# Second mixture of a two-layer transformer on one core: expert passes with the hidden units on partitions, bias and rectifier in one instruction, second bias by TensorE, expert words kept in registers, deviation per block, 39 blocks

## The reference, cut to what matters

```python
h = relu(einsum('bld,edh->eblh', x, W1) + b1)        # x is the layer-normed input
y = einsum('eblh,ehd->ebld', h, W2) + b2
gate = softmax(x @ gate_W + gate_b);  vals, idx = top_k(gate, 2)
out0 = y of expert idx[0] for x;  out1 = y of expert idx[1] for x + 0.5 * out0
result = layer_norm(x + vals[0] * out0 + vals[1] * out1, gamma, beta, eps=1e-5)
```

## Time and profile before

| what | value |
|---|---|
| median of 3 runs | 1687.01 us (1680.38 to 1689.57) |
| profiled execution | 1688.53 us, span 1686.7 us |
| `route_gate` | about 1391 to 1487 us |
| pass 0, entry to the last scatter's end | 1487.9 to 1571.2 us |
| pass 1, entry to the last scatter's end | 1577.2 to 1680.3 us |
| end of the program | 1686.7 us |
| busy share of the span | PE 85%, DVE 65%, ACT 51%, POOL 41% |

### The profile page before, as it was taken

The page is one execution under the profiler, slowest core; times in us unless marked ns, Lnnn a source line. Parts: engine busy times, 40 slices in busy tenths (PEclk is TensorE's granted clock), DMA queues, the critical chain, the costliest instruction groups (busy, mean ns, idle before and its releaser), DMA issues. The chain is left out here.

```text
span 1686.7 us, 36701 instructions
## 1 busy us (share of the span) xinstructions
PE 1428.5 (85%) x12500; PEld 940.8 (56%) x12500; DVE 1094.9 (65%) x2690; ACT 858.2 (51%) x1437; POOL 684.8 (41%) x1037
## 2 busy tenths in 40 slices
PE   3799999999999979989999548999999985058583
PEld 1255555555555547669999514555566655046452
DVE  3778778788787726744444447888888745336483
ACT  1567677776766656314444214566666654023242
POOL 2223242332323111463333256566653214635287
PEclk8699999999999989999999867999999995579796
DMA  4111211212112003701212133333332202444341
GB/s 128 57 47 35 64 52 34 66 38 61 51 34 66 20 28 125 101 14 48 49 48 49 30 76 83 76 88 79 78 80 70 72 7 99 144 137 152 88 122 44
DMA packets 92373, 115.54 MB, mean 68 GB/s; under 512 B 13090, under 2 KB 75841, under 8 KB 91936
## 3 DMA queue, kind: packets, MB, share of 16 engines
q1 hardware_dynamic: 75360, 91.63, 19.7%
q0 software_dynamic: 16832, 21.56, 5.6%
HBM read 73.67 MB, written 39.21 MB: 67 GB/s over the span
## 5 line engine op out<-in xcount | busy, mean ns | idle before, releaser
L688 DVE TENSOR_REDUCE wm<-wsm 128x16 f32<-128x512 f32 x512 | 330.1, 685 | 112.7 <-PE wsm L428 109.7
L585 ACT ACTIVATE we<-wst 128x1024 f32<-128x1024 f32 x320 | 325.1, 1022 | 120.0 <-PE wst L461 109.0
L585 ACT ACTIVATE ce<-cst 128x896 f32<-128x896 f32 (+1 forms) x256 | 172.6, 704 | 136.2 <-PE cst L456 116.9
L684 DVE TENSOR_REDUCE cnm<-csm 128x1 f32<-128x512 f32 (+3 forms) x352 | 213.1, 636 | 42.9 <-PE csm L425 37.0
L428 PE MATMUL wsm<-wks,wqs 96*128 96x512 bf16 x512 | 173.4, 394 | 9.1 <-DVE wm L688 5.6
L461 PE MATMUL wst<-wqs,wks 128*128 128x512 bf16 x512 | 149.8, 384 | 0.3 <-ACT we L585 0.3
L1718 PE MATMUL abup<-abxt,abws 128*128 128x128 f32 x1120 | 138.7, 278 | 0.4 <-ACT abxt L1744 0.4
L421 PE MATMUL csm<-cks,cqs 96*128 96x256 bf16 (+3 forms) x512 | 131.5, 309 | 6.9 <-DVE cnm L684 5.0
L1718 PEld LDWEIGHTS abup<-abxt,abws 128*128 128x128 f32 x1120 | 132.6, 194 | 0.7 <-ACT abxt L1744 0.7
L495 PE MATMUL woa<-we,wv 128*32 128x128 f32 (+2 forms) x2560 | 130.6, 340 | 0.0
L814 POOL TENSOR_TENSOR wdif<-wglb,wloc 128x16 f32<-128x16 f32 x32 | 7.1, 221 | 290.2 <-DVE wloc L710 290.2
(11 more groups left out here) (327 smaller groups left out, 3037.1 us busy)
## 6 DMA issues: line engine op xcount, KB each, us to landing
wqs<-qk_parts SPq DMA_DIRECT2D x96, 96.0 KB
wks<-qk_parts SPq DMA_DIRECT2D x96, 96.0 KB
cqs<-qk_parts SPq DMA_DIRECT2D x96, 96.0 KB
cks<-qk_parts SPq DMA_DIRECT2D x96, 96.0 KB
b1r<-rows SPq DMA_DIRECT2D x40, 194.0 KB
qk_parts<-wpt SPq DMA_DIRECT2D x48, 128.0 KB
qk_parts<-cpt SPq DMA_DIRECT2D x48, 128.0 KB
b0r<-rows SPq DMA_DIRECT2D x40, 130.0 KB
```

The costliest lines, as they stand in the source:

```text
L585: act.activation(E[:, e_slot(g, i), 0:width], ST[:, (U * g + i) % 2, 0:width], ACT.Exp, scale=SCALE).then_inc(s_ex, 1)
L684: dve.tensor_reduce(NM[:, n % 2, first:first + heads, t], got, AX.X, ALU.max).then_inc(s_mx, 1)
L688: dve.tensor_reduce(M[:, n % 2, hs, t, :].rearrange("p (w f) -> p w f", f=DIL), SM[:, j % 2, :].rearrange("p (w i f) -> p w f i", w=NT, f= ...
```

## The change

Only `mixture1` and what it calls changes, and the host's layout of the first bias, which is now stored as 128 x 16: unit on partition, expert and half along the free axis.

- **Units on partitions.** ScalarE copies the block's expert's W1 (128 x 256) to a fixed place `WS`. TensorE uses its halves as stationary side, so that `UP` holds 128 units on partitions and 128 rows along the free axis, once per half. The turning (`TH`, L2092) and `HH` go.
- **Bias and rectifier in one.** Per half one instruction makes relu(UP + b1) straight into `HT`. In pass 0 half 0 is VectorE's and half 1 ScalarE's; in pass 1 both are ScalarE's.
- **Second bias by TensorE.** A third matmul, ones times a `B2` whose rows but the first are zero, starts the sum in `Y`. `YB` goes.
- **Words in registers.** TensorE and ScalarE (and VectorE in pass 0) load all 10 words before their first block.
- **Deviation per block.** ScalarE takes sqrt(var + eps), VectorE the reciprocal, and VectorE multiplies with it and adds x + beta in one instruction. `power`, the multiplication on ScalarE and the addition on GpSimd go. GpSimd only scatters.
- **39 blocks** in place of 40.

```diff
-        B1 = sb("b1", [P, NE1, F1])
+        B1 = sb("b1", [P, NE1, HB1])
...
-            sp.dma_start(B1[:, :, :], b1.rearrange("e h -> (e h)").partition_broadcast(P)).then_inc(s_w, 16)
-            sp.dma_start(B2[:, :, :], b2.rearrange("e d -> (e d)").partition_broadcast(P)).then_inc(s_w, 16)
+            sp.dma_start(B1[:, :, :], b1.rearrange("h (e c) -> h e c", c=HB1)).then_inc(s_w, 16)
+            sp.wait_ge(s_b2, 1)
+            sp.dma_start(B2[0:1, :, :], b2.rearrange("(a e) d -> a e d", a=1)).then_inc(s_w, 16)
...
+            pool.memset(B2[:, :, :], 0.0).then_inc(s_b2, 1)
...
-    N = BLOCKS1
+    N = USED1
...
+        def words(eng):
+            return [word(eng, at) for at in range(-(-N // UN))]
...
+            known = words(pe)
             turn_rows(0)
+            for i in range(N + 1):
+                if i + 1 < N:
+                    turn_rows(i + 1)
+                if i < N:
+                    pe.wait_ge(s_ws, i + 1)
+                    pe.wait_ge(s_xt, i + 1)
+                    for c in range(HB):
+                        if i > 1:
+                            pe.wait_ge(s_h[c], i - 1)
+                        m = pe.matmul(UP[:, i % 2, c, 0:P], WS[:, i % 2, c * P:(c + 1) * P], XT[:, i % 2, :], start=True,
+                                      stop=True)
+                    m.then_inc(s_up, 1)
+                if i > 0:
+                    j = i - 1
+                    e = expert(known, j)
+                    if j > 1:
+                        pe.wait_ge(s_z if final else s_bo, j - 1)
+                    pe.matmul(Y[:, j % 2, 0:D], const["ones"], B2[:, bass.ds(e * D, D)], start=True, stop=False)
+                    for c in range(HB):
+                        pe.wait_ge(s_h[c], j + 1)
+                        m = pe.matmul(Y[:, j % 2, 0:D], HT[:, j % 2, c, :], W2[:, bass.ds(e * HB * D + c * D, D)],
+                                      start=False, stop=(c == HB - 1))
+                    m.then_inc(s_y, 1)
...
+            known = words(act)
+            for i in range(-1, N + 3):
+                if i + 1 < N:
+                    j = i + 1
+                    e = expert(known, j)
+                    if j > 1:
+                        act.wait_ge(s_up, j - 1)
+                    act.copy(WS[:, j % 2, :], W1[:, bass.ds(e * F, F)]).then_inc(s_ws, 1)
+                    act.wait_ge(s_tx, j + 1)
+                    act.copy(XT[:, j % 2, :], TX[:, j % 2, 0:P]).then_inc(s_xt, 1)
+                if 0 <= i < N:
+                    act.wait_ge(s_up, i + 1)
+                    if i > 1:
+                        act.wait_ge(s_y, i - 1)
+                    for c in ON_ACT:
+                        act.activation(HT[:, i % 2, c, :], UP[:, i % 2, c, 0:P], ACT.Relu, bias=bias(known, i, c)
+                                       ).then_inc(s_h[c], 1)
+                if final and 0 <= i - 3 < N:
+                    j = i - 3
...
+                    act.wait_ge(s_mv, j + 1)
...
+                    act.activation(std[:, j % K:j % K + 1], mv[:, j % K, 1:2], ACT.Sqrt, bias=eps[:, :]).then_inc(s_sd, 1)
...
+                if final and 0 <= i - 4 < N:
+                    j = i - 4
+                    dve.wait_ge(s_sd, j + 1)
+                    dve.reciprocal(rstd[:, j % K:j % K + 1], std[:, j % K:j % K + 1]).then_inc(s_rs, 1)
...
+                    dve.scalar_tensor_tensor(z0(q), z0(q), rstd[:, j % K:j % K + 1], R[:, q, IN_XB:IN_XB + D], ALU.mult,
+                                             ALU.add).then_inc(s_o, 1)
```

More of the change, by code:

```diff
@@ L1051 @@
 BLOCKS1 = 40
+USED1 = 39
 OUT_W = D
@@ L2046, in word, with expert, bias @@
             return eng.value_load(table[0:1, at:at + 1], min_val=0, max_val=(1 << 18) - 1)
-        def expert(word, place):
-            return (word >> (EBITS * (place + 2))) & (TOP - 1)
+        def words(eng):
+            return [word(eng, at) for at in range(-(-N // UN))]
+        def expert(words, i):
+            return (words[i // UN] >> (EBITS * (i % UN + 2))) & (TOP - 1)
         def z0(q):
             return R[:, q, Z0:Z0 + D]
+        def bias(words, i, c):
+            return B1[:, bass.ds(expert(words, i) * HB + c, 1)]
         @block.sync
@@ L2071, in turn_rows @@
                 pe.transpose(TX[:, i % 2, 0:P], R[:, i % Q, 0:D], const["ident"]).then_inc(s_tx, 1)
+            known = words(pe)
             turn_rows(0)
-            for i in range(N + 2):
-                if i % UN == 0:
-                    now = word(pe, i // UN)
-                if i < N:
-                    pe.wait_ge(s_xt, i + 1)
-                    if i > 1:
-                        pe.wait_ge(s_h, i - 1)
-                    e = expert(now, i % UN)
-                    pe.matmul(UP[:, i % 2, 0:F], XT[:, i % 2, :], W1[:, bass.ds(e * F, F)], start=True, stop=True
-                              ).then_inc(s_up, 1)
+            for i in range(N + 1):
@@ L2094, in _ @@
-                    m.then_inc(s_th, 1)
-                if 0 <= i - 2 < N:
-                    j = i - 2
-                    e = expert(now, i % UN - 2)
-                    pe.wait_ge(s_ht, j + 1)
-                    if j > 1:
-                        pe.wait_ge(s_yb, j - 1)
-                    for c in range(HB):
-                        m = pe.matmul(Y[:, j % 2, 0:D], HT[:, j % 2, c * P:(c + 1) * P],
-                                      W2[:, bass.ds(e * HB * D + c * D, D)], start=(c == 0), stop=(c == HB - 1))
+                        pe.wait_ge(s_h[c], j + 1)
@@ new lines, in _ @@
+        @block.vector
+        def _(dve):
+            if final:
+                dve.memset(eps[:, :], EPS).then_inc(s_eps, 1)
+            else:
+                known = words(dve)
+            for i in range(N + 5):
+                if not final and i < N:
+                    dve.wait_ge(s_up, i + 1)
+                    if i > 1:
+                        dve.wait_ge(s_y, i - 1)
+                    dve.tensor_scalar(HT[:, i % 2, 0, :], UP[:, i % 2, 0, 0:P], bias(known, i, 0), 0.0, ALU.add, ALU.max
+                                      ).then_inc(s_h[0], 1)
+                if final and 0 <= i - 4 < N:
+                    j = i - 4
+                    dve.wait_ge(s_sd, j + 1)
+                    dve.reciprocal(rstd[:, j % K:j % K + 1], std[:, j % K:j % K + 1]).then_inc(s_rs, 1)
+                if final and 0 <= i - 2 < N:
+                    j = i - 2
+                    dve.wait_ge(s_z, j + 1)
+                    dve.bn_stats(stats[:, j % 4, :], z0(j % Q)).then_inc(s_bn, 1)
+                if final and 0 <= i - 3 < N:
+                    j = i - 3
+                    dve.wait_ge(s_mv, j + 1)
+                    dve.scalar_tensor_tensor(z0(j % Q), z0(j % Q), mv[:, j % K, 0:1], GA[:, :], ALU.subtract, ALU.mult
+                                             ).then_inc(s_u, 1)
+                if final and 0 <= i - 2 < N:
+                    j = i - 2
+                    dve.wait_ge(s_bn, j + 1)
+                    dve.bn_aggr(mv[:, j % K, :], stats[:, j % 4, :]).then_inc(s_mv, 1)
+                if final and 0 <= i - 4 < N:
+                    j = i - 4
+                    q = j % Q
+                    dve.wait_ge(s_u, j + 1)
+                    dve.wait_ge(s_rs, j + 1)
+                    dve.scalar_tensor_tensor(z0(q), z0(q), rstd[:, j % K:j % K + 1], R[:, q, IN_XB:IN_XB + D], ALU.mult,
+                                             ALU.add).then_inc(s_o, 1)
@@ L2207, in _ @@
                     pool.wait_ge(s_bo, i + 1)
-                    scatter(i)
+                scatter(i)
             for q in range(Q):
```

112 lines of the change are left out of this document (26 added, 86 removed).

## The result

| | before | changed |
|---|---|---|
| median | 1685.78 us (1680.38 to 1689.57) | 1669.30 us (1664.31 to 1671.81) |
| profiled execution, span | 1688.53, 1686.7 us | 1671.81, 1669.8 us |
| pass 0, SP's first load to the end of the last scatter | 82.4 us | 82.0 us |
| pass 1, the same | 102.2 us | 87.2 us |

The ratio is 0.9899, interval 0.9879 to 0.9919. The gain is 1.0% where I had forecast 2.7%, and it lies outside my range: 1669 against 1629 to 1664. Pass 1 gained 15.0 us, pass 0 0.4.

What follows compares the result with a forecast made beforehand. Pass 1 was taken as bound by GpSimd, pass 0's middle by a chain of waits. Pass 0 -15.6 and pass 1 -30.7, together -46.3 on 1688.5, gave 1642.2, or 1641 us as median; range 1629 to 1664.

Steps and rivals of the forecast that it cites:

- the 0.11 us a block for late moments: Pass 0: whole pipeline 0.9 us late about every 14 us, 8 blocks; kept unchanged as 0.11 us a block.
- TensorE's block, 1.23: Both passes at full clock: a transpose and five matmuls, 0.11 + 5 x 0.223 = 1.23 us a block.
- The middle of pass 0, 1.40 forecast: Pass 0 at full clock: slowest of 1.23 and 1.28 plus 0.11, so 1.40 us a block, 34 blocks 47.6 us.
- ScalarE's 1.40 as the bound of pass 1: Pass 1: ScalarE's copies, halves, root and 0.08 of uncovered register arithmetic take 1.40 us; plus 0.10 gives 1.50 a block.
- VectorE 1.3 to 1.4: Pass 1: VectorE's block falls from 1.60 to 1.3 to 1.4 us, with the 0.62 us word stops gone.
- GpSimd's 1.26 to 1.30: Both passes: scatters that wait for nothing take 0.96 + 0.30, so 1.26 to 1.30 us a block.
- The words: Entry of each pass: ten loads ahead of the first block delay the first transpose by 3.3 us (bounds +2 and +4).
- The start: Each pass: half clock at 2.46 us a block, 9.4 us from the transpose in pass 0; then block 4 at full clock.
- The tails: End of each pass, from block 38's first product to the last scatter's end: 3.6 us in pass 0, 5.0 in pass 1.
- The table load: Pass 1, ScalarE's square root: 1.28 us once, in block 3 at half clock, costing nothing there, 1.3 us at most.
- the latency rival: Both passes: waits between engines still set the pace, 1.65 and 1.75 us a block, 1658 us (1650 to 1672); chance 0.28.
- GpSimd alone sets the pace: Rival, both passes: late moments swallowed by TensorE's longer queue, 1.29 and 1.35 us a block, 1632 us; chance 0.15.

Runs made afterwards that it cites:

- direct: Kernel before, scatters of both passes replaced by direct transfers from SP's queue (rows to wrong places): 1651.09 us, ratio 0.9806.
- with memset: Kernel before, a GpSimd memset of 128x388 put behind each scatter of pass 0: 1681.00 us, ratio 0.9971.
- the version with the third product: Changed kernel plus one more TensorE matmul per block, into columns nobody reads: 1678.73 us, ratio 0.9959.
- the direct version: Changed kernel, each GpSimd scatter replaced by one direct transfer from SP's queue (rows to wrong places): 1618.34 us, ratio 0.9603.
- the 388-column memset: Changed kernel, GpSimd memset of 128x388 behind every scatter: 1653.4 us with words loaded at entry, 1649.2 us with words loaded where needed.
- 512 columns: Changed kernel, words loaded where needed, GpSimd memset of 128x512 behind every scatter: 1654.2 us, ratio 0.9814.

## Why the prediction failed

**The step that failed is the 0.11 us a block for late moments, "which I leave as they are".** It measured 1.80 - 1.23 = 0.57 in pass 0 and 1.85 - 1.26 = 0.59 in pass 1 over the pace without scatters, or 0.51 and 0.56 over the scatter's 1.29. I had taken the lag of the earlier trace rows as a given of TensorE, at fixed times, and weighed instruction fetches for it. It depended on how closely GpSimd issues, and that is what the change moved. In pass 1 it took away the addition and the power between the scatters. In pass 0 the kernel before, word stops included, gives a block every 1.55 us (direct) to 1.58 (with memset), just at the edge of the table; the changed kernel could give one every 1.23, far inside it. (That the edge explains the difference is my reading; it fits both kernels and the version with the third product, which gives one every 1.45.) The term was too small even for the kernel before, where it is 1.77 - 1.55 = 0.22. The earlier trace rows stood for eight cases, and GpSimd's timeline of the kernel before, which I hadn't laid beside them, has three scatters back to back ahead of the first (the readers start at 1510.76):

```profile
1506.44 0.98 POOL L2179 DMA_INDIRECT rows<-b0r  x1 [0.89 <-DVE b0r L2169]
1507.73 1.07 POOL L2179 DMA_INDIRECT rows<-b0r  x1 [0.30 <-DVE b0r L2169]
1509.10 0.98 POOL L2179 DMA_INDIRECT rows<-b0r  x1 [0.30 <-issue]
```

The earlier trace rows had the 0.30 of gap.

By terms, where + is time lost against the forecast, against the measured gain of 15.4 us in the passes (46.3 forecast):

- TensorE's block, 1.23: right to the hundredth, 1.22 and 1.23.
- The middle of pass 0, 1.40 forecast, 1.80 measured: 34 x 0.40 = 13.6 us. Pass 1, 1.50 against 1.85: 11.9.
- ScalarE's 1.40 as the bound of pass 1: wrong, it is no bound. Its timeline in the direct version, one block of pass 1:

```profile
1591.02 0.27 ACT L2140 COPY b1xt<-b1tx 128x128 f32<-128x128 f32 x1
1591.24 0.62 ACT L2146 ACTIVATE b1ht<-b1up,bb 128x128 f32<-128x128 f32 x2
1591.76 0.29 ACT L2155 ACTIVATE b1std<-b1mv,b1eps 128x1 f32<-128x1 f32 x1
1591.95 0.40 ACT L2138 COPY b1ws<-bw 128x256 f32 x1
1592.24 0.27 ACT L2140 COPY b1xt<-b1tx 128x128 f32<-128x128 f32 x1
```

  From start to start 0.22 + 0.52 + 0.19 + 0.29 = 1.22. The halves take 0.26 each where I had 0.30, and no register arithmetic stands uncovered.
- VectorE 1.3 to 1.4: it fits into 1.23 in the direct version. GpSimd's 1.26 to 1.30: right, 0.99 + 0.30 within a run.
- The words: from SP's first load to the first transpose 2.13 us before and 5.76 after in pass 0, so +3.6 (forecast 3.3). But the term was worth nothing in the changed kernel, since loads where needed leave its time alone (1667.9), as the stalls eat what the start gives. Beside the 388-column memset the passes are 1.9 and 2.3 us shorter with them.
- The start: block 4's first product 16.5 and 16.4 us after the entry by the forecast, some 14.5 in both passes by the trace, since the half clock lasted about 6.5 us from the first transpose (1493.2 to some 1499.7) and not 9.4: -3.9, the words' extra 0.3 in it. (The 9.4 itself was read from the edge of a window; the trace of before has the rise at 1500.7, 9.8 us after the transpose.)
- The tails: 3.6 and 5.0 us forecast, 7.3 and 10.7 measured, +9.4; the blocks that a stall releases leave their scatters at the end.
- The table load lasts 1.28 us, as the earlier trace rows had it. It fell into block 4, at full clock, and not into one at half: TensorE waits 0.92 us for the weights there in the direct version, where I had taken 0. ScalarE's timeline of the changed kernel:

```profile
1590.00 1.28 ACT L2137 ACT_TABLE_LOAD   x1
1591.30 0.29 ACT L2137 ACTIVATE b1std<-b1mv,b1eps 128x1 f32<-128x1 f32 x1
```

  The next instruction follows 0.02 us after its end. The Trainium skill, "ScalarE: Activation LUTs", section on what a table load costs, adds a drain; the trace doesn't show one here.

The table load lies in pass 1's middle. The sum is 25.5 - 3.9 + 9.4 = 31.0 of the 30.9 us that were missing.

Of the rivals, the latency rival had the time (1650 to 1672), but by luck, for its reason is wrong: the cadence is not bound by latency, the direct version shows it at TensorE's own 1.23. GpSimd alone sets the pace only where its scatters are spaced: 1.69 us with 512 columns. The clock rose as forecast, and the order of the instructions is what the change says.

The Trainium skill, "Runtime: NRT & Kernel Launch", section on instruction fetch mechanics, says that a crossing is "mostly hidden". The trace agrees: with the same 106 fetches, the late moments are gone in the direct version, so they never were the crossings that I had weighed. The Trainium skill, "DMA: Bandwidth & Descriptors", section on SWDGE, HWDGE and iDMA, says that GpSimd builds the descriptors of its transfers itself, into SBUF, and that a transfer from SP's queue never touches this path. The direct version agrees as far as it goes: 1618 against 1669. The Trainium skill, "SBUF — State Buffer", section on the two separate sides, says that TensorE's and ScalarE's ports "never wait on anyone". That may hold of the ports; here TensorE's signals do come late beside GpSimd's scatters, by 1.8 to 2.9 us at most stops of pass 0.

**What stays open** is the way by which the scatters hold the signals. One reading fits the times: each scatter leaves some 1.43 us of work that is done in turn. From the start of a run of three to the release it is 1522.26 - 1517.94 = 4.32 us, three times 1.44, and with 388 columns 1.41 after a single one; by this reading scatters 1.47 and 1.53 apart would not pile up, though, and they stall, so it isn't the whole. No run separates the descriptors' writing from the transfers' end. A plain transfer issued by GpSimd was not run, nor an indirect one to neighbouring rows, so the direct version alone doesn't say whether the issuer, the indirection or the scattered places matter; the memsets, which change only the spacing, say that GpSimd's timing is part of it. The profile models the ends of matmuls, so a late signal can't be told from a late last write; TensorE itself goes on meanwhile (in the stop shown, with 11 matmuls after the transpose of 1519.46). Whether signals of other engines are held as well was not tried, and that chips differ was seen and not explained.

## What to carry to other kernels

Look at what GpSimd was doing at each unexplained late moment of TensorE's readers, and price it anew when a change moves GpSimd's issues closer: here the pace that the other engines allow fell from 1.55 to 1.23 us a block, past an edge between 1.53 and 1.58, and the scatters took half of the gain. If indirect transfers must follow each other, put other GpSimd work between them, here 0.46 us, so that they start 1.6 us apart or more (by what was measured here), and take a plain transfer from SP where the addresses allow it. And run a version that suddenly beats all its neighbours once more before you believe it: two chips differed in this by more than the change was worth (1638 and 1661).

## What the runs showed of the hardware that I had not expected

- GpSimd's indirect scatters of 128 rows, 1.29 to 1.53 us from start to start, hold TensorE's signals to ScalarE and VectorE: in pass 0 of the changed kernel mostly for 1.8 to 2.9 us, in the kernel before for 0.6 to 1.3. At 1.58 they still do in stretches, for 0.5 to 2.0 us, with few stalls; at 1.69 no copy was late. One chip had a single stall in two passes at a mean of 1.49. The same blocks from SP's queue hold nothing.
- A memset of 128 columns on GpSimd costs 0.24 us and lengthens the gap between two scatters by 0.08 only; 0.16 of it lies in the 0.30 that passes between them anyway.
- The same kernel took 1638.4 us on one chip and 1661.3 on another (5 runs each, 1637.5 to 1640.3 and 1659.7 to 1666.9), the kernel before 1676.3 and 1687.0.
